# Attention in a graph network: exponentials and clips taken two tiles at a time

## The reference

```python
q = (embeds[rows] @ qW).reshape(e, HEADS, dh)
k = (embeds[cols] @ kW).reshape(e, HEADS, dh)
v = (embeds[cols] @ vW).reshape(e, HEADS, dh)
scores = jnp.clip(jnp.einsum('ehd,ehd->eh', q, k), -10.0, 10.0)
exp_s = jnp.exp(scores)
norms = jax.ops.segment_sum(exp_s, rows, num_segments=nvar)[rows]
w = exp_s / (norms + 1e-08)
res = jax.ops.segment_sum(w[:, :, None] * v, rows, num_segments=nvar).reshape(nvar, d)
return embeds + res
...
h = jnp.maximum(_layernorm(x, axis=-1), 0.0)
x = x + _L0_gnn_ref(h, L0_gnn_qW, L0_gnn_kW, L0_gnn_vW, src, dst)
```

## Time and profile before

| what | us |
|---|---|
| median of 3 runs (2825.99 to 2841.65) | 2830.38 |
| span of the profiled execution | 3436.4 |
| attention, in that span | 218 to 714 |

### The profile page before, as it was taken

One profiled execution on the slowest core, in us unless ns is written; L12 is line 12 of the kernel. 1 busy time (PEld: TensorE's weight loads), 2 busy tenths in 40 slices (PEclk: granted clock), 3 DMA queues, 4 the chain that ended last, 5 costly groups with the idle time before them and its releaser, 6 DMA issues. The chain is left out here.

```text
span 3436.4 us, 72105 instructions
## 1 busy us (share of the span) xinstructions
PE 3216.7 (94%) x29232; PEld 2446.7 (71%) x29232; DVE 1807.0 (53%) x5033; ACT 1163.4 (34%) x2585; POOL 1106.3 (32%) x1407
## 2 busy tenths in 40 slices
PE   7989999978999995799999848999999999999999
PEld 4667777745666664466666637988888888888888
DVE  7977777765777772477777630042322222222223
ACT  5976666653434442243444420031110111110110
POOL 4037777735555554355555521000000000000000
PEclk6556666656666665666666656666666666666666
DMA  5020000034444454254444527800000000000000
GB/s 167 2 80 11 9 10 10 10 99 102 119 120 123 124 124 107 62 128 123 124 119 122 159 82 218 260 5 1 1 1 1 1 1 1 1 1 1 1 1 15
DMA packets 147170, 227.40 MB, mean 66 GB/s; under 512 B 55568, under 2 KB 112619, under 8 KB 146162
## 3 DMA queue, kind: packets, MB, share of 16 engines
q1 hardware_dynamic: 120350, 184.69, 18.4%
q0 software_dynamic: 22944, 36.72, 5.4%
q10 hardware_dynamic: 3540, 1.30, 0.1%
HBM read 122.26 MB, written 100.35 MB: 65 GB/s over the span
## 5 line engine op out<-in xcount | busy, mean ns | idle before, releaser
L1884 POOL DMA_INDIRECT max_row<-table,max_src_rows x640 | 641.8, 1003 | 557.0 <-PE max_col L1900 284.1
L1911 PE MATMUL max_far<-adj 128*96 128x512 f16 x1800 | 713.4, 513 | 3.7 <-DVE adj L2033 2.4
L2378 PE MATMUL prop<-g,adj 128*128 128x192 f16 x4608 | 568.1, 307 | 6.1 <-DVE g L2452 6.1
L2378 PE MATMUL prop<-weights_then_states,adj 128*128 128x192 f16 x4608 | 566.5, 307 | 0.0
L2378 PEld LDWEIGHTS prop<-g,adj 128*128 128x128 f16 x4608 | 498.2, 119 | 74.8 <-issue 11.6
L2378 PEld LDWEIGHTS prop<-weights_then_states,adj 128*128 128x128 f16 x4608 | 497.4, 119 | 68.0 <-issue 5.9
L2486 DVE SCALAR_TENSOR_TENSOR support_parts<-prop,coef,weights_then_states 128x96 f32<-128x96 f32 x384 | 120.6, 314 | 677.2 <-PE prop L2378 534.8
L1756 POOL TENSOR_SCALAR e<-e 128x512 f32<-128x512 f32 (+1 forms) x625 | 366.5, 604 | 273.6 <-ACT e L1744 272.4
L2033 DVE TENSOR_SCALAR adj<-adj,node_numbers 128x512 f16<-128x512 f16 x900 | 323.4, 362 | 246.5 <-PE max_far L1911 180.2
L1770 DVE TENSOR_TENSOR e<-e,a_ps 128x1024 f32<-128x1024 f32 (+1 forms) x313 | 373.6, 1194 | 127.1 <-PE a_ps L1682 122.6
L1744 ACT ACTIVATE e<-s_ps 128x512 f32<-128x512 f32 (+1 forms) x625 | 336.1, 585 | 155.2 <-PE o_ps L1694 150.6
(11 more groups left out here) (287 smaller groups left out, 3717.3 us busy)
## 6 DMA issues: line engine op xcount, KB each, us to landing
weights_then_states<-weights SPq DMA_DIRECT2D x100, 400.0 KB, 4.0
weights<-max_rows_w SPq DMA_DIRECT2D x52, 400.0 KB
rows_dram<-max_out SPq DMA_DIRECT2D x100, 192.0 KB
weights<-adj SPq DMA_DIRECT2D x48, 400.0 KB
max_same<-same_dram SPq DMA_DIRECT2D x196, 96.0 KB
rows_dram<-adj SPq DMA_DIRECT2D x96, 192.0 KB
max_row<-table,max_src_rows POOLq DMA_INDIRECT x640
adj<-ids_dram SPq DMA_DIRECT2D x36, 128.0 KB
```

What stands on the lines that cost most here:

```text
L1884: nc.gpsimd.indirect_dma_start(row[i % RING][:, j, :], None, table_dram, bass.IndirectOffsetOnAxis(ap=src_rows[:, 4 * n + j:4 * n + j + 1] ...
L1911: mm = nc.tensor.matmul(far_ps[j % 2][0:D, :], parts[:, k, a, :], hot[(T * j + k) % HOTS], start=k == a == 0, stop=k == T - 1 and a == 1)
L2378: return nc.tensor.matmul(sums(step, t), adj[:, k, t * P:(t + 1) * P], states[:, k, :], start=start and t % 2 == 0, stop=k == END - 1 and ...
```

## The change

An exponential and a clip now take a pair of tiles in one instruction each, 128 x 2 x 512 values instead of 128 x 512. The four score banks become two pairs of banks, and an exponential reads both banks of a pair. Each semaphore that counted tiles for these (`exped`, `clipped`) counts pairs, and the waits follow: the exponential waits for the scores of both tiles, and for the values of both tiles of the pair three earlier; the scores of a pair wait for the exponential of the pair two earlier; the weights wait for one clip. Scores, masks, weights and values keep their number, size and order.

```diff
--- before.py
+++ after.py
@@ -1599,7 +1599,7 @@
 def attention(nc, c, adj, q_st, v_all, qk_dram, res_dram, away_dram):
-    S_RINGS, E_PAIRS = 4, 3
+    S_PAIRS, E_PAIRS = 2, 3
     AHEAD, MASK_AHEAD = 6, 2
     TILES = T * T
     PAIRS = -(-TILES // 2)
@@ -1616,7 +1616,7 @@
         res = o_sb[:, 0:HEADS * (DH + 1)]
         first_exp = sb("first_exp", [P, 1], F32)
-        s_ps = [ctx.enter_context(nc.psum_tensor(f"s_ps{i}", [P, 512], F32)) for i in range(S_RINGS)]
+        s_ps = [ctx.enter_context(nc.psum_tensor(f"s_ps{i}", [P, 2, 512], F32)) for i in range(S_PAIRS)]
         a_ps = [ctx.enter_context(nc.psum_tensor(f"a_ps{i}", [P, 1024], F16)) for i in range(2)]
         o_ps = [ctx.enter_context(nc.psum_tensor(f"o_ps{i}", [P, 512], F32)) for i in range(2)]
         turned_at = slice(256, 256 + HEADS * VW)
@@ -1630,6 +1630,7 @@
         block = ctx.enter_context(nc.Block())
         e_tile = lambda u: e[:, u // 2 % E_PAIRS, u % 2, 0:HEADS * width(u // T)]
+        e_pair = lambda p: e[:, p % E_PAIRS, 0:len(tiles_of(p)), 0:HEADS * width(2 * p // T)]
         @block.sync
         def _(sp):
@@ -1665,11 +1666,11 @@
                     pe.wait_ge(q_loaded[row % 2], 64 * (row // 2))
                 if row == 0 and t in key_parts:
                     pe.wait_ge(k_loaded[key_parts[t]], 64)
-                if u >= S_RINGS:
-                    pe.wait_ge(exped, u - S_RINGS + 1)
+                if u % 2 == 0 and u // 2 >= S_PAIRS:
+                    pe.wait_ge(exped, u // 2 - S_PAIRS + 1)
                 for hd in range(HEADS):
-                    mm = nc.tensor.matmul(s_ps[u % S_RINGS][:, hd * w:(hd + 1) * w], k_st[:, hd, t * P:(t + 1) * P],
+                    mm = nc.tensor.matmul(s_ps[u // 2 % S_PAIRS][:, u % 2, hd * w:(hd + 1) * w], k_st[:, hd, t * P:(t + 1) * P],
                                           q_st[:, row % 2, hd, 0:w], start=True, stop=True)
                 mm.then_inc(scored, 1)
@@ -1735,25 +1736,27 @@
                 nc.scalar.activation(res.rearrange("p (h f) -> p h f", h=HEADS), sums[:, :, 0:DH + 1], ACT.Copy).then_inc(res_ready, 1)
             nc.scalar.activation(first_exp[:, :], c.ones[:, 0:1], ACT.Exp)
-            for u in range(TILES):
-                row, t = divmod(u, T)
-                act.wait_ge(scored, u + 1)
-                if u >= 2 * E_PAIRS:
-                    act.wait_ge(summed, u - 2 * E_PAIRS + 1)
-                nc.scalar.activation(e_tile(u), s_ps[u % S_RINGS][:, 0:HEADS * width(row)], ACT.Exp).then_inc(exped, 1)
-                if t == 8 and row >= 1:
-                    keep(row - 1)
-                if t == 14 and row >= 1:
-                    keep_turned(row - 1)
+            for p in range(PAIRS):
+                tiles = tiles_of(p)
+                act.wait_ge(scored, tiles[-1] + 1)
+                if p >= E_PAIRS:
+                    act.wait_ge(summed, 2 * (p - E_PAIRS) + 2)
+                nc.scalar.activation(e_pair(p), s_ps[p % S_PAIRS][:, 0:len(tiles), 0:HEADS * width(tiles[0] // T)], ACT.Exp).then_inc(exped, 1)
+                for u in tiles:
+                    row, t = divmod(u, T)
+                    if t == 8 and row >= 1:
+                        keep(row - 1)
+                    if t == 14 and row >= 1:
+                        keep_turned(row - 1)
             keep(T - 1)
             keep_turned(T - 1)
         @block.gpsimd
         def _(pool):
-            for u in range(TILES):
-                pool.wait_ge(exped, u + 1)
-                nc.gpsimd.tensor_scalar(e_tile(u), e_tile(u), math.exp(10.0), math.exp(-10.0), ALU.min, ALU.max).then_inc(clipped, 1)
+            for p in range(PAIRS):
+                pool.wait_ge(exped, p + 1)
+                nc.gpsimd.tensor_scalar(e_pair(p), e_pair(p), math.exp(10.0), math.exp(-10.0), ALU.min, ALU.max).then_inc(clipped, 1)
             pool.wait_ge(res_stored, 16 * (T - 1))
             nc.gpsimd.memset(o_sb[:, LAST:P], 0.0).then_inc(o_cleared, 1)
@@ -1763,7 +1766,7 @@
             def weight(p):
                 dve.wait_ge(masked, p + 1)
                 tiles = tiles_of(p)
-                dve.wait_ge(clipped, tiles[-1] + 1)
+                dve.wait_ge(clipped, p + 1)
                 w, n = width(tiles[0] // T), len(tiles)
                 tile = e[:, p % E_PAIRS, 0:n, 0:HEADS * w].rearrange("p a (h n) -> p a h n", h=HEADS)
                 a = a_ps[p % 2][:, 0:n * P].rearrange("p (a n) -> p a n", n=P)[:, :, 0:w]
```

## The result

| | us |
|---|---|
| before, median of 4 runs | 2832.01 |
| after, median of 4 runs | 2884.81 |
| ratio after / before | 1.0179, 95% interval 1.0151 to 1.0207 |

The changed kernel is 1.8% slower, +52.8 us between the medians; the forecast was 2880 us, +50. The ratio times 2832 gives +51. Attention begins at 218 us in a later profile of before and in that of after; its last store starts at 619.2 us in the one and 666.2 in the other, so the loss lies in attention.

What follows compares the result with a forecast made beforehand. PE bounds the profile, but at the timed runs' full clock the three-place ring does: 300 pairs x (1.41 - 1.24) = +51, short pairs and later end +2, copies -3, so +50, 2880 us; range 2851 to 2902.

Steps and rivals of the forecast that it cites:

- The clock of the timed runs: Attention's granted clock in timed runs: inferred between 0.81 and 1.0, taken as 1.0, against 0.65 in the profile.
- 606 us: Profiled span of 3436.4 us less the timed median of 2830.4 us, read as a higher clock in timed runs.
- 1.49 under PE's 1.60: Attention at the profile's clock: the new ring's 1.49 us a pair stays hidden under PE's 1.60, costing nothing.
- no change: Rival: attention stays PE-bound in the timed runs, at a clock of 0.71 or less; 2830 us, chance 0.14.
- The ring: Attention: exponential, clip, weight, values of one of e's three places; 3.71 to 4.22 us, 1.24 to 1.41 a pair.
- the slopes: Time per element from instructions of 512 and 212 elements: 0.83 ns exponential, 0.84 clip; paired, 1.02 and 1.04 us.
- Score banks: Scores on PE wait once per pair for the exponential two pairs earlier: cover 0.17 us, cost nothing.
- Copies: Copies of keep and keep_turned between exponentials on ACT: better hidden after the change, at most 6 us back, 3 taken.
- No engine needs as much alone: Attention before, full clock: PE 1.05, DVE 1.13 to 1.22, POOL 1.19, ACT 1.08 a pair, under the ring's 1.24.
- My expectation for four places: Attention with a fourth place in e: ring 0.93 a pair, DVE binds at 1.14 to 1.22, 15 to 35 us shorter.
- faster: Rival: POOL's hand-overs bind before, so a merged clip lets DVE's 1.22 lead; -15, 2815 us, chance 0.11.
- worse: Rival: the two wide instructions cost what two did, 1.08 and 1.19; 2902 us, chance 0.75 together with the forecast.

Runs made afterwards that it cites:

- four places: Kernel before with a fourth place for pairs in e from pair 39 on, rows attended in another order: 0.9972 of before.
- the clips alone: Kernel before with only the clips taken in pairs, each waiting for the second exponential; exponentials stay by tile: 1.0105 of before.
- the kernels with four places: Before and changed kernel with a fourth place in e: 0.9972, 0.9983 of before; the former with fewer scores, a single run: 2804.9 us.

## Why the prediction was right

- **The clock of the timed runs** was inferred from 606 us, and held: attention runs at 1.00 in every profile after the first, and every run that is listed with the experiments, of before and of the other kernels, has a mean granted clock of 0.890 to 0.906, where the first profile had 0.636. The trace that the rows came from was of a case in which, by the prediction's sum (1.49 under PE's 1.60), the change would have cost nothing; no run of the changed kernel at that clock shows it. Reading only its stage would have given "no change".
- **The ring** was the cause, link by link:

| link, us | forecast before, after | measured before, after |
|---|---|---|
| values to exponential | 0.46, 0.70 | 0.55, 0.77 |
| exponential to clip | 0.68, 1.10 | 0.68, 1.10 |
| clips | 1.19, 1.04 | 1.19, 1.04 |
| clip to weight | 0.10, 0.10 | 0.10, 0.11 |
| weight to values | 1.28, 1.28 | 1.28, 1.27 |
| sum | 3.71, 4.22 | 3.80, 4.29 |

  The measured columns are differences of the starts in the two timelines of one passage above, except that the clips are their duration and clip to weight counts from its end. Their sums differ by 0.49, forecast 0.51; over three pairs and 300 full pairs that is 49 us. Only the first link was off, by 0.07 to 0.09 in both columns, so it hardly touches the difference: I scaled all of the values' 0.74 us with the clock, and they take 0.57 at 1.00, not 0.48. That accounts for the link of after (0.57 + 0.22 = 0.79) and for half of the error before (0.29 + 0.22 = 0.51, measured 0.55); the rest is open.
- **Where it comes from.** Over 300 pairs the links of the two passages give +22 us for the later first exponential, +42 for the overlap that was lost between the second exponential and the first clip, and -15 for the single clip. The first of these has a kernel of its own: the wait for both tiles alone brings 23 us. The third does not stand out of the noise of the times (58 us without the single clip, 51 with it); it rests on the paces, 1.48 and 1.43.
- **Instructions.** 1.02 and 1.04 us, as worked out from the slopes.
- **Score banks** and their wait cost nothing that shows, as costed.
- **Copies**: with them the pace is 1.27 before, where the passage without a copy gives 1.27 too, and 1.43 after. The 3 us that I gave them can't be told from nothing.
- **The step that was wrong** did no harm here, and that is luck: "No engine needs as much alone" took PE's pair at 1.05 at the full clock. It is 1.24, so before the change PE stood 0.03 below the ring and not 0.19. Had it stood above 1.27, it would have set the pace before, and the loss would have been smaller than the difference of the rings. A longer ring of places could therefore give back the loss but hardly more. My expectation for four places, 15 to 35 us, failed by this.
- **The rivals** are out: no change by the clock of 1.00 and by PE's 246.46 busy us of 270 in the changed kernel, faster by the clips alone and by the kernels with four places, where two clips a pair keep up at 1.24 and 1.15, and worse by 1.02 and 1.04.

Four places with tiles one by one are the fastest of the whole kernels by the point value, 0.9972 of before with an interval that ends at 0.9996; so small a gain is hardly clear of the noise, and it needs another order of the rows.

## What to carry to other kernels

Where a few buffers go round through several engines, count the time of one passage and divide by the buffers before grouping instructions: an engine that idles gains nothing from fewer instructions, while a grouped step starts later and ends later for whoever is next. Here grouping cost nothing once the passage over the number of places, 4.29 / 4 = 1.07 us, fell below the next bound, PE's 1.24; so look first for room for one more buffer. And compare a profile's span with the timed runs: where they differ, the bound that the profile shows may not be theirs.

## What the runs showed of the hardware

- PE's pair did not shrink as the clock: from 1.60 us at a granted 0.65 to 1.24 at 1.00 with four places, a factor of 0.78 where the clocks stand as 0.65. The two mask transposes take 0.12 in both, the scores 0.74 and 0.55, the values 0.74 and 0.57. Why is open; the semaphore wait ahead of the masks isn't it.
- The same kernel was profiled once at a steady 0.65 and once at 1.00 in the PE-bound stretches, 3436.4 and 2852.2 us, with nothing in the program to tell why; the record does not say on which chip the first was taken, so the chip stays a possible cause. The first value is neither 1.2 nor 2.4 GHz.
